# Binary convolution branch in jobs of 784 pixels on all four 64x64 corners of TensorE, with a scalar operand in the ratio

## Chip, core and metric

One NeuronCore of a Trainium2 chip runs the whole program. The metric is the time of one execution on the device in microseconds (us); lower is better.

## What is computed

The input `x` is (32, 64, 56, 56) in float32. Two blocks follow each other, each with a residual. The first is a binary convolution branch: the signs of the group-normed input go through a 3x3 depthwise convolution with sign weights, PReLU, batch norm and sign, a 1x1 convolution with sign weights, PReLU and batch norm. The second is an involution: a 1x1 convolution (64 to 576 channels, float32) makes nine filter taps per pixel, and these are multiplied with the nine shifted copies of the group-normed input and summed.

```python
def _L0(x):                       # x is already group-normed
    h = sign(x)
    h = depthwise3x3(h, sign(dw_weight))
    h = sign(bn1(prelu1(h)))
    h = einsum('bchw,oc->bohw', h, sign(pw_weight))
    return bn2(prelu2(h)) + x

def _L1(x):
    f = einsum('bchw,oc->bohw', x, W) + b        # 9 taps per channel
    return sum_k(patch_k(x) * f[:, :, k])

x = x + _L0(gn(x))                # gn: 32 groups of 2 channels
x = x + _L1(gn(x))
```

## The kernel before

A **tile** is two images, 128 partitions (image 0 on partitions 0 to 63, image 1 on 64 to 127, one channel per partition) by 3136 pixels. There are 16 tiles. The engines' programs are written by hand: a loop over steps, in each of which one tile is `taps` (its involution runs), the next one is `mid`, the one after that `front`, and one is being loaded. Inside a step there are 36 **units** `u`: four **quarters** of the image (784 pixels in two halves of 392), nine taps each. Every engine runs through the same units in order, and each piece of work has a unit at which it stands in an engine's queue; a delay such as `PW_DELAY` is a distance in units. Units count on from a step into the next, where `front` becomes `mid`.

**Involution.** For unit `u` TensorE (`unit`, L340) makes one tap of 784 pixels with four float32 matmuls, one in each 64x64 corner of the array (each stands as two records in the trace), into one of `SLOTS = 3` PSUM slots of `tap_ps`. VectorE (`product`, L667) adds the bias and multiplies it with the shifted `q`. Unit `u` may start only when product `u - 3` has ended (L347); where that product is the ninth tap of a quarter, it waits for `pair` (L692) instead, a sum that VectorE runs after the first product of the next quarter:

```python
before = t.count(UNITS, u - SLOTS)
if before % KK == PAIR_K:
    wait(pe, paired, before // KK + 1)
else:
    wait(pe, prod_done, before + 1)
```

Counting the units of a quarter from 0 to 8, `pair` stands behind product 0 of the next quarter, and unit 2 of that quarter waits for it. GpSimd sums the products of a quarter (L270 to L304), partly through an accumulating DMA.

**Convolution branch.** It works in 8 **chunks** of 392 pixels. For a chunk, TensorE runs nine depthwise taps of two matmuls (`depthwise`, L359), each in its own diagonal corner, so that both images run side by side, into `dw_ps`. ScalarE makes two sign planes `ab` from it (`conv_act`, L427). TensorE multiplies both with the 1x1 weights into `pw_ps` (`pointwise`, L375), ScalarE applies a ReLU in place (`relu_act`, L434), TensorE adds the planes once more (`add_h`, L384), and VectorE adds the result to `xb` in place with a sum for the next norm (`x1_sum`, L653). A chunk starts every 4 units; `dw_ps` and `pw_ps` are one bank each and `ab` has two buffers. In each engine's queue the piece for unit `u` of TensorE comes behind `unit(u)`, and `x1_sum` on VectorE comes ahead of `product(u)`.

**Statistics.** ScalarE makes the sums (`sum0`, `square0`, `sum1`, `square1`), VectorE exchanges partner channels with small shuffles, GpSimd takes the power. VectorE also makes `ratio` (L648), a 128x1 product of two operands in SBUF. `q_pass` and `q_half` on ScalarE write the normed `q`, and eight copies (`mirror_half`, L213) bring the other image's half to each side before the tile's taps start.

Of the kernel before, what the change touches and what calls it, by code (L numbers as in the profile page):

```python
# [18 lines left out]
def preact_involution_kernel(nc, x, dw, a1, gam1, bet1, mu1, var1, pw, a2, gam2, bet2, mu2, var2, W, b, out):  # L19
# [12 lines left out]
    SLOTS = 3  # L32
    N_GROUP = 2 * NPIX
# [8 lines left out]
    with ExitStack() as ctx:  # L42
# [8 lines left out]
        signs = sb("signs", [P, HP, WP], BF16)  # L51
# [34 lines left out]
        dw_ps = ctx.enter_context(nc.psum_tensor("dw_ps", [P, 512], F32))  # L86
        pw_ps = ctx.enter_context(nc.psum_tensor("pw_ps", [P, 512], F32))
# [13 lines left out]
        sums = sb("sums", [P, 2, CHUNKS], F32)  # L101
        scaled = sb("scaled", [P, CHUNKS], F32)
# [75 lines left out]
        def chunks_due(u, delay, mid, front):  # L178
            return due(u, delay, FIRST_CHUNK, CHUNK_EVERY, CHUNKS, front, mid)

# [140 lines left out]
        def _(pe):  # L321
            pe.wait_ge(ident_ready, 1)
            pe.wait_ge(signs_ready, 3)
            pe.matmul(dw_ps[:, 0:P], pw_block[:], ident_bf[:], start=True, stop=True)
            pe.matmul(dw_ps[:, P:2 * P], pw_block[:], ident_sg[:], start=True, stop=True).then_inc(pw_turned, 1)
            pe.wait_ge(pwk_ready, 1)
            pe.matmul(pw_ps[:, 0:1], pw_k[:], minus_k_terms[:], start=True, stop=True).then_inc(k_ready, 1)
# [31 lines left out]
            def depthwise(t, c, taps):  # L359

                if c == 0 and taps.start == 0:
# [12 lines left out]

            def pointwise(t, c):  # L375
                pe.wait_ge(ab_done, t.count(CHUNKS, c + 1))
                wait(pe, x1_done, t.count(CHUNKS, c))
                for n, pw_n in enumerate((pw_a, pw_b)):
                    for side in range(2):
                        own = slice(side * C, side * C + C)  # L380
                        mm = pe.matmul(pw_ps[own, 0:CH], pw_n[own, own], ab[own, c % 2, n, :], start=(n == 0), stop=(n == 1))  # L381
                mm.then_inc(pw_ready, 1)

            def add_h(t, c):  # L384

                pe.wait_ge(relu_done, t.count(CHUNKS, c + 1))
                for n, pw_n in enumerate((pw_a_sg, pw_b_sg)):
                    for side in range(2):
                        own = slice(side * C, side * C + C)
                        mm = pe.matmul(pw_ps[own, 0:CH], pw_n[own, own], ab[own, c % 2, n, :], start=False, stop=(n == 1),  # L390
                                       skip_group_check=True)
                mm.then_inc(h_ready, 1)

            def step(done, taps, mid, front, load):
                for u in range(UNITS):
# [6 lines left out]
                    for t, c in chunks_due(u, 0, mid, front):  # L402
                        depthwise(t, c, range(0, 5))
                    for t, c in chunks_due(u, 1, mid, front):
                        depthwise(t, c, range(5, KK))
                    for t, c in chunks_due(u, PW_DELAY, mid, front):
                        pointwise(t, c)
                    for t, c in chunks_due(u, ADD_H_DELAY, mid, front):
                        add_h(t, c)
# [4 lines left out]
        def _(act):  # L414
# [12 lines left out]
            def conv_act(t, c):  # L427

                act.wait_ge(dw_ready, t.count(CHUNKS, c + 1))
                wait(act, h_ready, t.count(CHUNKS, c - 1))  # L430
                acts(ab[:, c % 2, 0, :], dw_ps[:, 0:CH], ACT.Sign, scale=c_(A_SC), bias=c_(A_BI))
                acts(ab[:, c % 2, 1, :], dw_ps[:, 0:CH], ACT.Sign, scale=c_(B_SC), bias=c_(B_BI)).then_inc(ab_done, 1)

            def relu_act(t, c):  # L434
                act.wait_ge(pw_ready, t.count(CHUNKS, c + 1))
                acts(pw_ps[:, 0:CH], pw_ps[:, 0:CH], ACT.Relu, scale=c_(NEG_D), bias=c_(NEG_DK)).then_inc(relu_done, 1)
# [12 lines left out]
            def sum1(t):  # L449

                act.wait_ge(x1_done, t.count(CHUNKS, CHUNKS))
# [16 lines left out]
            def sign0(t):  # L468
                wait(act, dw_ready, t.count(CHUNKS))
                acts(signs[:, 1:1 + H, 1:1 + WD], rows3(xb[:, t.slot, :]), ACT.Sign, bias=s_(t, NM0)).then_inc(signs_done, 1)  # L470

            def scales0(t):
# [8 lines left out]
                acts(s_(t, HALF_B), s_(t, ZB), ACT.Copy, scale=-0.5 / CHUNKS)  # L481
# [30 lines left out]
            def step(done, taps, mid, front, load):  # L512
                for u in range(UNITS):
                    for t, c in chunks_due(u, AB_DELAY, mid, front):
                        conv_act(t, c)
                    for t, c in chunks_due(u, PW_DELAY, mid, front):
                        relu_act(t, c)
# [271 lines left out]
```

## Time and profile before

| what | value |
|---|---|
| median of 3 runs | 834.75 us (833.67 to 837.43) |
| the profiled execution | 835.78 us, its span 833.9 us |
| VectorE busy | 747.3 us, 90% |
| TensorE busy | 702.7 us, 84% |
| GpSimd busy | 573.4 us, 69% |
| ScalarE busy | 518.5 us, 62% |

The span has three stretches. Up to 88.6 us there is no involution work: tile 0 and part of tile 1 go through the convolution branch. From 88.6 to 761.9 us 58 quarters of the involution run with convolution work beside them. The last 6 quarters, up to 823.1 us, have none, and 11 us of closing work follow. Busy shares over the whole span mix these.

### The profile page before, as it was taken

To read this page: it belongs to the slowest core of one execution; us is meant where nothing else is said; L and a number is where in the kernel's file an instruction comes from. 1 tells how busy PE (TensorE), PEld (TensorE's weight loads), DVE (VectorE), ACT (ScalarE), POOL (GpSimd) and SP (SyncE) were. 2 spreads that over 40 slices of the span, in tenths; PEclk is the share of its full clock that TensorE was granted. 3 is DMA by queue.
4 is the path that set the end of the run, shared out by engine and by line. 5 is a ranking of instruction groups with operands and counts; after the bars stand their busy time and mean duration, and the time that the engine had idled before them with its cause. 6 is when DMAs were issued, how large, how long until landed. Compare 5 with 4: busy or idle time off the path is not lost.

```text
span 833.9 us, 19099 instructions
## 1 busy us (share of the span) xinstructions
PE 702.7 (84%) x7975; PEld 404.2 (48%) x7975; DVE 747.3 (90%) x1136; ACT 518.5 (62%) x772; POOL 573.4 (69%) x393
## 2 busy tenths in 40 slices
PE   0766889899998989998999989998999989897783
PEld 0323556455555555554555555554555555552221
DVE  6211799999999999999999999999999999999998
ACT  4586876667676767667685767766675767633000
POOL 2000167878787787878687786878787777778885
PEclk9988999999999999999999999999999999999986
DMA  5101559798887979698888889697988888686983
GB/s 205 44 1 31 140 115 248 149 210 192 173 219 160 235 147 246 139 233 170 210 182 173 215 163 247 140 238 159 217 180 171 212 172 165 142 174 143 198 165 95
DMA packets 40023, 142.14 MB, mean 170 GB/s; under 512 B 5248, under 2 KB 13440, under 8 KB 37888
## 3 DMA queue, kind: packets, MB, share of 16 engines
q0 software_dynamic: 17296, 75.87, 50.7%
q1 hardware_dynamic: 22640, 65.04, 23.4%
q8 instruction: 63, 1.03, 0.5%
q14 instruction: 24, 0.20, 0.1%
HBM read 25.86 MB, written 25.69 MB: 62 GB/s over the span
## 4 chain that ended last, share of the span: by engine, by line
DVE 56%; PE 32%; issue 6%; ACT 5%; DMA 1%; SPq 0%; DVEq 0%
DVE prod L685 35%; PE tap_ps L356 18%; PE dw_ps L369 11%; DVE prod L697 7%; DVE tap_ps L685 6%; DVE xb L659 4%; PE pw_ps L390 2%; ACT ab L416 2%; DVE st L651 1%; ACT unused L416 1%; PE pw_ps L381 1%; DVE st L555 1%; DMA prod<-prod 1%; ACT signs L416 1%; DVE prod L705 0%
## 5 line engine op out<-in xcount | busy, mean ns | idle before, releaser
L356 PE MATMUL tap_ps<-q,w_t 64*64 64x392 f32 x2304 | 466.9, 500 | 63.6 <-DVE prod L697 61.3
L356 PE MATMUL tap_ps<-mirror,w_t 64*64 64x392 f32 x2304 | 479.9, 517 | 0.0
L685 DVE SCALAR_TENSOR_TENSOR prod<-tap_ps,bias,q 128x784 f32<-128x784 f32 x448 | 452.3, 1029 | 11.5 <-PE tap_ps L356 7.3
L369 PE MATMUL dw_ps<-signs,dw_diag 64*64 64x392 bf16 x2304 | 246.3, 335 | 16.0 <-ACT ab L416 13.6
L416 ACT ACTIVATE ab<-dw_ps,col 128x392 bf16<-128x392 f32 x256 | 158.5, 669 | 160.0 <-PE dw_ps L369 160.0
L356 PEld LDWEIGHTS tap_ps<-q,w_t 64*64 64x64 f32 x2304 | 171.8, 134 | 166.9 <-DVE prod L697 95.8
L369 PEld LDWEIGHTS dw_ps<-signs,dw_diag 64*64 64x64 bf16 x2304 | 146.3, 108 | 139.2 <-issue 81.4
L282 POOL TENSOR_TENSOR prod<-prod 128x784 f32<-128x784 f32 x63 | 117.0, 1857 | 90.3 <-DVE prod L697 90.3
L289 POOL TENSOR_TENSOR prod<-prod 128x784 f32<-128x784 f32 x63 | 139.7, 2218 | 27.6 <-DMA prod<-prod 27.6
L356 PEld LDWEIGHTS tap_ps<-mirror,w_t 64*64 64x64 f32 x2304 | 124.6, 133 | 2.2
L304 POOL TENSOR_TENSOR ob<-prod 128x784 f32<-128x784 f32 x63 | 116.8, 1854 | 10.6 <-POOL prod L295 10.3
L295 POOL TENSOR_TENSOR prod<-prod 128x784 f32<-128x784 f32 x63 | 116.5, 1849 | 0.0
L659 DVE SCALAR_TENSOR_TENSOR xb<-pw_ps,st,xb 128x392 f32<-128x392 f32 x128 | 79.1, 618 | 39.8 <-PE pw_ps L390 39.2
L274 POOL DMA_DIRECT2D prod<-prod x63 | 76.4, 1213 | 54.3 <-DVE prod L685 54.3
L416 ACT ACTIVATE pw_ps<-pw_ps,col 128x392 f32<-128x392 f32 x128 | 82.7, 646 | 30.7 <-PE pw_ps L381 30.7
L416 ACT ACTIVATE unused<-xb,st 128x3136 bf16<-128x3136 f32 x32 | 94.6, 2955 | 1.1
L685 DVE SCALAR_TENSOR_TENSOR tap_ps<-tap_ps,bias,q 128x784 f32<-128x784 f32 x64 | 66.3, 1036 | 4.1 <-PE tap_ps L356 4.1
L685 DVE SCALAR_TENSOR_TENSOR prod<-tap_ps,st,q 128x784 f32<-128x784 f32 x64 | 65.9, 1030 | 4.4 <-PE tap_ps L356 4.0
L697 DVE SCALAR_TENSOR_TENSOR prod<-tap_ps,st,prod 128x784 f32<-128x784 f32 x64 | 65.7, 1026 | 0.0
L381 PE MATMUL pw_ps<-ab,pw_a 64*64 64x392 bf16 x256 | 44.9, 331 | 14.2 <-ACT ab L416 9.8
L416 ACT ACTIVATE q<-xb,st 128x1568 f32<-128x1568 f32 x32 | 52.6, 1692 | 0.5
L259 POOL TENSOR_SCALAR st<-st 128x1 f32<-128x1 f32 x32 | 9.5, 297 | 56.4 <-DVE st L555 53.6
(101 smaller groups left out, 464.2 us busy)
## 6 DMA issues: line engine op xcount, KB each, us to landing
prod<-prod POOLq DMA_DIRECT2D x63, 1176.0 KB, 10.3
xb<-in_x_dram SPq DMA_DIRECT2D x16, 1568.0 KB, 11.7
out_dram<-ob SPq DMA_DIRECT2D x64, 392.0 KB, 2.9
mirror<-q SPq DMA_DIRECT2D x128, 101.5 KB, 4.6
prod<-prod SPq DMA_DIRECT2D x1, 146.2 KB, 2.3
prod<-in_L_conv_W_dram SPq DMA_DIRECT2D x1, 144.0 KB, 6.3
prod<-prod SPq DMA_DIRECT2D x1, 20.8 KB, 6.1
prod<-in_L_conv_prelu_a_dram SPq DMA_DIRECT2D x1, 0.2 KB, 2.3
```

Source lines behind the costliest of these rows:

```text
L274: pool.dma_start(prod[:, g % BUFS, 3:6, :], prod[:, g % BUFS, 0:3, :], accum_op=ALU.add, max_dma_last_dim=6 * QP).then_inc(folded[g % BUFS ...
L282: pool.tensor_tensor(pr[6], pr[6], pr[7], ALU.add).then_inc(summed67, 1)
L289: pool.tensor_tensor(pr[4], pr[4], pr[5], ALU.add).then_inc(summed45, 1)
L295: pool.tensor_tensor(pr[3], pr[3], pr[6], ALU.add).then_inc(summed36, 1)
L304: pool.tensor_tensor(ob[:, qq % 2, :], pr[3], pr[4], ALU.add).then_inc(summed, 1)
L356: mm = pe.matmul(rows3(tap_ps[to, u % SLOTS, side, 0:CH]), w_t[own, k, :], moving, start=True, stop=True)
L369: mm = pe.matmul(rows3(dw_ps[own, 0:CH]), dw_diag[own, k, own], signs[own, c * ROWS + dy:c * ROWS + dy + ROWS, dx:dx + WD], start=(k == 0) ...
L381: mm = pe.matmul(pw_ps[own, 0:CH], pw_n[own, own], ab[own, c % 2, n, :], start=(n == 0), stop=(n == 1))
L416: return nc.scalar.activation(o, i, f, **kw)
L659: v.scalar_tensor_tensor(xc, pw_ps[:, 0:CH], s_(t, RATIO), xc, ALU.mult, ALU.add, accum_out=sums[:, t.par, c:c + 1]).then_inc(x1_done, 1)
L685: v.scalar_tensor_tensor(place.rearrange("p j (a b) -> p j a b", b=WD), psum.rearrange("p j (a b) -> p j a b", b=WD), s_(t, B4) if k == 4 ...
L697: v.scalar_tensor_tensor(into, tap_ps[:, (KK * g + PAIR_K) % SLOTS, :, 0:CH], s_(t, MEAN1), into, ALU.add, ALU.add).then_inc(paired, 1)
```

## The change

The branch works in 4 **jobs** of 784 pixels instead of 8 chunks of 392. A job is two chunks. In `depthwise` the image picks the rows of the array and the PSUM bank, and the chunk picks the columns, that is the output partitions: all four corners work on one tap, with the same number of matmuls in all. In `pointwise` and `add_h` the roles are exchanged back: the chunk picks rows and bank, the image the columns. One PSUM tensor `conv_ps` of two banks takes the place of `dw_ps` and `pw_ps` and serves a job from its first depthwise tap to `x1_sum`; `ab` has one buffer. ScalarE and VectorE work on 784 pixels per instruction. Each job's nine taps stand in three units instead of two. `signs` has a buffer for each parity of the tile. `ratio` takes its second operand as a per-partition scalar. The places of all pieces in the queues are new.

```diff
-        dw_ps = ctx.enter_context(nc.psum_tensor("dw_ps", [P, 512], F32))
-        pw_ps = ctx.enter_context(nc.psum_tensor("pw_ps", [P, 512], F32))
+        conv_ps = ctx.enter_context(nc.psum_tensor("conv_ps", [P, 2, 512], F32))
...
-            def depthwise(t, c, taps):
+            def depthwise(t, j, taps):
...
                 if taps.start == 0:
-                    wait(pe, ab_done, t.count(CHUNKS, c))
+                    wait(pe, x1_done, t.count(JOBS, j))
                 for k in taps:
                     dy, dx = divmod(k, 3)
-                    for side in range(2):
-                        own = slice(side * C, side * C + C)
-                        mm = pe.matmul(rows3(dw_ps[own, 0:CH]), dw_diag[own, k, own],
-                                       signs[own, c * ROWS + dy:c * ROWS + dy + ROWS, dx:dx + WD],
-                                       start=(k == 0), stop=(k == KK - 1))
+                    for image in range(2):
+                        own = slice(image * C, image * C + C)
+                        for chunk in range(2):
+                            to = slice(chunk * C, chunk * C + C)
+                            first = (2 * j + chunk) * ROWS + dy
+                            mm = pe.matmul(rows3(conv_ps[to, image, 0:CH]), dw_diag[own, k, own],
+                                           signs[own, t.par, first:first + ROWS, dx:dx + WD],
+                                           start=(k == 0), stop=(k == KK - 1))
...
+                pe.wait_ge(ab_done, t.count(JOBS, j + 1))
                 for n, pw_n in enumerate((pw_a, pw_b)):
+                    for chunk in range(2):
+                        own = slice(chunk * C, chunk * C + C)
+                        for image in range(2):
+                            to = slice(image * C, image * C + C)
+                            mm = pe.matmul(conv_ps[to, chunk, 0:CH], pw_n[own, own], ab[own, n, image, :],
+                                           start=(n == 0), stop=(n == 1))
...
+                    for part in range(3):
+                        for t, j in jobs_due(u, part, mid, front):
+                            depthwise(t, j, range(3 * part, 3 * part + 3))
...
-                v.tensor_tensor(s_(t, RATIO), s_(t, INVZ), c_(S2_SG), ALU.mult).then_inc(ratio_done, 1)
+                v.tensor_scalar(s_(t, RATIO), s_(t, INVZ), c_(S2_SG), None, ALU.mult).then_inc(ratio_done, 1)
...
-                v.scalar_tensor_tensor(xc, pw_ps[:, 0:CH], s_(t, RATIO), xc, ALU.mult, ALU.add,
-                                       accum_out=sums[:, t.par, c:c + 1]).then_inc(x1_done, 1)
+                xj = xb[:, t.slot, j * QP:(j + 1) * QP].rearrange("p (a n) -> p a n", a=2)
+                v.scalar_tensor_tensor(xj, conv_ps[:, :, 0:CH], s_(t, RATIO), xj, ALU.mult, ALU.add,
+                                       accum_out=sums[:, t.par, j:j + 1]).then_inc(x1_done, 1)
...
-FIRST_CHUNK = 13
-CHUNK_EVERY = 4
-PW_DELAY = 6
-AB_DELAY = 2
-X1_DELAY = 9
-ADD_H_DELAY = 8
+FIRST_JOB = 20
+JOB_EVERY = 9
+AB_DELAY = 3
+PW_DELAY = 5
+RELU_DELAY = 6
+ADD_H_DELAY = 7
+X1_DELAY = 5
...
-SUM1_AT = 18
-MEAN1_AT = 15
-SQUARE1_AT = 18
+SUM1_AT = 19
+MEAN1_AT = 18
+SQUARE1_AT = 20
 VAR1_AT = 21
-R1_AT = 23
-Q_AT = (23, 26)
+R1_AT = 22
+Q_AT = (27, 28)
```

## Rows read from the trace of the kernel before

**Rows 1.** Busy us (x instructions), clock, DMA share, GB/s, by stretch.

```profile
core 0: us, PE busy (x) PEld busy (x) DVE busy (x) ACT busy (x) POOL busy (x), PEclk, DMA share, GB/s
33.00:55.00 22.00, 14.49 (x150) 7.30 (x146) 4.01 (x16) 15.55 (x22) 0.29 (x1) 1.00 0.00 1
...
100.00:740.00 640.00, 581.81 (x6835) 348.92 (x6830) 624.73 (x922) 441.21 (x661) 491.99 (x327) 1.00 0.83 188
```

**Rows 2.** Groups of instructions: busy us, mean ns of one, idle before.

```profile
L685 DVE SCALAR_TENSOR_TENSOR prod<-tap_ps,bias,q 128x784 f32<-128x784 f32 x448 | 452.3, 1029 | 11.5 <-PE tap_ps L356 7.3
L416 ACT ACTIVATE ab<-dw_ps,col 128x392 bf16<-128x392 f32 x256 | 158.5, 669 | 160.0 <-PE dw_ps L369 160.0
L659 DVE SCALAR_TENSOR_TENSOR xb<-pw_ps,st,xb 128x392 f32<-128x392 f32 x128 | 79.1, 618 | 39.8 <-PE pw_ps L390 39.2
L416 ACT ACTIVATE pw_ps<-pw_ps,col 128x392 f32<-128x392 f32 x128 | 82.7, 646 | 30.7 <-PE pw_ps L381 30.7
L416 ACT ACTIVATE unused<-xb,st 128x3136 bf16<-128x3136 f32 x32 | 94.6, 2955 | 1.1
...
L665 DVE RECIPROCAL st<-st 128x1 f32<-128x1 f32 x16 | 2.4, 153 | 0.0
```

**Rows 3.** VectorE in order of time: start us, us, what.

```profile
307.02 0.62 DVE L659 SCALAR_TENSOR_TENSOR xb<-pw_ps,st,xb 128x392 f32<-128x392 f32 x1
...
307.56 1.04 DVE L685 SCALAR_TENSOR_TENSOR tap_ps<-tap_ps,bias,q 128x784 f32<-128x784 f32 x1
...
309.56 1.03 DVE L697 SCALAR_TENSOR_TENSOR prod<-tap_ps,st,prod 128x784 f32<-128x784 f32 x1
310.50 2.13 DVE L685 SCALAR_TENSOR_TENSOR prod<-tap_ps,bias,q 128x784 f32<-128x784 f32 x2
```

**Rows 4.** TensorE in order of time, the same place.

```profile
310.63 0.54 PE L356 MATMUL tap_ps<-q,w_t 64*64 64x392 f32 x1 [1.17 <-DVE prod L697]
310.64 0.55 PE L356 MATMUL tap_ps<-mirror,w_t 64*64 64x392 f32 x2
...
311.35 1.02 PE L369 MATMUL dw_ps<-signs,dw_diag 64*64 64x392 bf16 x10
...
312.19 0.33 PE L390 MATMUL pw_ps<-ab,pw_a_sg 64*64 64x392 bf16 x1
...
315.17 0.51 PE L356 MATMUL tap_ps<-q,w_t 64*64 64x392 f32 x2
...
315.83 0.51 PE L356 MATMUL tap_ps<-q,w_t 64*64 64x392 f32 x2
```

**Rows 5.** The ratio's instruction alone: duration ns min/median/max.

```profile
L651 DVE TENSOR_TENSOR st<-st,col x16: 160/1794/1809, 24.8 to 717.6; 128x1 f32<-128x1 f32 x16
```

**Rows 6.** VectorE: the first products, and the sums L697 that close quarters.

```profile
88.62 1.98 DVE L685 SCALAR_TENSOR_TENSOR prod<-tap_ps,bias,q 128x784 f32<-128x784 f32 x2 [1.45 <-PE tap_ps L356]
...
760.87 1.03 DVE L697 SCALAR_TENSOR_TENSOR prod<-tap_ps,st,prod 128x784 f32<-128x784 f32 x1
...
801.92 1.03 DVE L697 SCALAR_TENSOR_TENSOR prod<-tap_ps,st,prod 128x784 f32<-128x784 f32 x1
...
812.34 1.03 DVE L697 SCALAR_TENSOR_TENSOR prod<-tap_ps,st,prod 128x784 f32<-128x784 f32 x1
```

**Rows 7.** TensorE in a late quarter without convolution work.

```profile
803.00 0.54 PE L356 MATMUL tap_ps<-q,w_t 64*64 64x392 f32 x1 [1.94 <-DVE prod L697]
...
804.40 0.87 PE L356 MATMUL tap_ps<-mirror,w_t 64*64 64x392 f32 x2
...
805.06 0.87 PE L356 MATMUL tap_ps<-mirror,w_t 64*64 64x392 f32 x2
```

**Rows 8.** The same quarter by stretches, columns as in rows 1.

```profile
804.00:806.00 2.00, 2.00 (x16) 0.81 (x13) 1.63 (x2) 0.00 (x0) 2.00 (x2) 0.50 1.02 179
```

**Rows 9.** TensorE: the first chunk's taps and the first tap unit.

```profile
23.31 3.15 PE L369 MATMUL dw_ps<-signs,dw_diag 64*64 64x392 bf16 x18 [2.13 <-ACT signs L416]
...
87.45 0.55 PE L356 MATMUL tap_ps<-mirror,w_t 64*64 64x392 f32 x2
```

More of the change, by code:

```diff
@@ L50, in preact_involution_kernel @@
         xb = sb("xb", [P, RING, NPIX], F32)
-        signs = sb("signs", [P, HP, WP], BF16)
+        signs = sb("signs", [P, 2, HP, WP], BF16)
         q = sb("q", [P, 2, HP, WP], F32)
@@ L372, in depthwise, with pointwise @@
                 if taps.stop == KK:
                     mm.then_inc(dw_ready, 1)
-            def pointwise(t, c):
-                pe.wait_ge(ab_done, t.count(CHUNKS, c + 1))
-                wait(pe, x1_done, t.count(CHUNKS, c))
+            def pointwise(t, j):
+                pe.wait_ge(ab_done, t.count(JOBS, j + 1))
                 for n, pw_n in enumerate((pw_a, pw_b)):
-                    for side in range(2):
-                        own = slice(side * C, side * C + C)
-                        mm = pe.matmul(pw_ps[own, 0:CH], pw_n[own, own], ab[own, c % 2, n, :], start=(n == 0), stop=(n == 1))
+                    for chunk in range(2):
[4 more added lines that the diff above has]
+                                           start=(n == 0), stop=(n == 1))
@@ L382, in pointwise, with add_h @@
                 mm.then_inc(pw_ready, 1)
-            def add_h(t, c):
-                pe.wait_ge(relu_done, t.count(CHUNKS, c + 1))
+            def add_h(t, j):
+                pe.wait_ge(relu_done, t.count(JOBS, j + 1))
                 for n, pw_n in enumerate((pw_a_sg, pw_b_sg)):
[L388 to L391, printed above, removed]
+                    for chunk in range(2):
+                        own = slice(chunk * C, chunk * C + C)
+                        for image in range(2):
+                            to = slice(image * C, image * C + C)
+                            mm = pe.matmul(conv_ps[to, chunk, 0:CH], pw_n[own, own], ab[own, n, image, :],
+                                           start=False, stop=(n == 1), skip_group_check=True)
@@ L401, in step @@
                         unit(taps, u)
[L402 to L409, printed above, removed]
+                    for part in range(3):
+                        for t, j in jobs_due(u, part, mid, front):
+                            depthwise(t, j, range(3 * part, 3 * part + 3))
+                    for t, j in jobs_due(u, PW_DELAY, mid, front):
+                        pointwise(t, j)
+                    for t, j in jobs_due(u, ADD_H_DELAY, mid, front):
+                        add_h(t, j)
             program(step)
@@ L425, in s_, with conv_act, relu_act @@
                 return st[:, t.slot, n:n + 1]
[L427 to L436, printed above, removed]
+            def conv_act(t, j):
+                act.wait_ge(dw_ready, t.count(JOBS, j + 1))
+                acts(ab[:, 0, :, :], conv_ps[:, :, 0:CH], ACT.Sign, scale=c_(A_SC), bias=c_(A_BI))
+                acts(ab[:, 1, :, :], conv_ps[:, :, 0:CH], ACT.Sign, scale=c_(B_SC), bias=c_(B_BI)).then_inc(ab_done, 1)
+            def relu_act(t, j):
+                act.wait_ge(pw_ready, t.count(JOBS, j + 1))
+                acts(conv_ps[:, :, 0:CH], conv_ps[:, :, 0:CH], ACT.Relu, scale=c_(NEG_D), bias=c_(NEG_DK)).then_inc(relu_done, 1)
             def sum0(t):
@@ L468, in sign0 @@
             def sign0(t):
-                wait(act, dw_ready, t.count(CHUNKS))
-                acts(signs[:, 1:1 + H, 1:1 + WD], rows3(xb[:, t.slot, :]), ACT.Sign, bias=s_(t, NM0)).then_inc(signs_done, 1)
+                wait(act, dw_ready, t.count(JOBS, -JOBS))
+                acts(signs[:, t.par, 1:1 + H, 1:1 + WD], rows3(xb[:, t.slot, :]), ACT.Sign, bias=s_(t, NM0)).then_inc(signs_done, 1)
             def scales0(t):
@@ L513, in step @@
                 for u in range(UNITS):
[L514 to L517, printed above, removed]
+                    for t, j in jobs_due(u, AB_DELAY, mid, front):
+                        conv_act(t, j)
+                    for t, j in jobs_due(u, RELU_DELAY, mid, front):
+                        relu_act(t, j)
                     if front:
@@ L717, in step @@
                         copy_w()
-                    for t, c in chunks_due(u, X1_DELAY, mid, front):
-                        x1_sum(t, c)
+                    for t, j in jobs_due(u, X1_DELAY, mid, front):
+                        x1_sum(t, j)
                     if taps:
```

52 lines of the change are left out of this document (26 added, 26 removed).

## Prediction

> **What bounds the kernel now.** I read the stretches first: from 100 to 740 us VectorE is busy for 624.73 of 640 us, 97.6%, more than any other engine [rows 1]. So in the long middle each microsecond that VectorE works or waits is one of the result; ScalarE (441) and TensorE (582, ends modelled) matter only where VectorE waits for them. Then I took prices from the groups [rows 2] and spacings from the order of time [rows 3, 4], because neighbours on VectorE overlap: x1_sum lasts 0.62 us but the next product starts 0.54 behind it; `pair` starts at 309.56 and the next product at 310.50, so both cost 0.94. The middle runs from 88.62 to the end of the `pair` at 760.87, 761.89: 58 quarters, 673.3 us, **11.61 us a quarter** [rows 6]. Of that, 9 x 0.943 + 0.945 + 2 x 0.54 = 10.5 is product, pair and x1_sum; the rest is small instructions, the ratio above all, and waits.
>
> **What it saves.** x1_sum: a product of 784 elements costs 0.41 us more than an x1_sum of 392 (1029 against 618 ns, both with a PSUM and an SBUF operand [rows 2]), so one of 784 costs 0.54 + 0.41 = 0.95 in place of 1.08: 0.13 a quarter. Ratio: 1794 ns in the median, 160 at its shortest [rows 5]. With a scalar operand only one tensor comes from SBUF; the nearest row with one such input is the reciprocal, 153 ns also in the middle [rows 2], so I take 0.15: 1.6 us a tile. Bounds: 0.15 and the old 1.8. The Trainium skill (SBUF — State Buffer, Who interferes with whom) says that VectorE's second read port is shared with GpSimd and that tensor_scalar can enter a mode that uses it; by that the ratio would still be held, and the sum would be some 15 us higher (an estimate: 14 tiles in the middle by 1.6 us, of which VectorE's waits at that place cover about a third). No row here has a tensor_scalar beside a busy GpSimd.
>
> TensorE: a depthwise tap of one chunk costs (312.19 - 311.35)/5 = 0.168 us for two corners [rows 4]. The tap units start matmuls in several corners within 0.01 us of each other (310.63, 310.64) and a whole unit of eight records takes 315.83 - 315.17 = 0.66 [rows 4], so four corners do run side by side in float32. I take 0.168 for four bf16 corners as well, bounds 0.168 and 0.336. A third of a job's taps is then 0.50, a pointwise or add_h of two passes 0.33. This halves TensorE's convolution work, but by itself is worth nothing while VectorE is the bound. ScalarE: (2955 - 669)/2744 = 0.83 ns an element [rows 2], so 392 more cost 0.33: the sign pair of a job 1.90 us, the ReLU 0.97.
>
> **What it adds: a wait in VectorE's own queue.** In units from a job's start, x1_sum now stands ahead of product 5, so VectorE comes to it when product 4 has ended. What it needs is add_h, which stands on TensorE behind unit 7. And unit 7 may start only when product 4 has ended. So VectorE stands still while TensorE runs unit 7 and add_h, whatever their speed. Before, x1_sum stood ahead of product 9 and add_h behind unit 8, which needs product 5 only: three products in between covered it. Behind the waiting x1_sum lie all products, and TensorE's unit 8 waits for them.
>
> I follow one quarter, with time 0 at the end of a `pair` and k the tap in the quarter. Jobs start at k = 2. Prices: TensorE starts 0.04 behind the release, a unit from rest holds it 0.72 (310.63 to 311.35), and VectorE can start 0.25 after a unit's stream (310.50 + 2.13 - 1.03 = 311.60 against 311.35) [rows 3, 4].
> - Unit 2 streams till 0.76; product 2 starts at 1.01, 0.15 later than back to back. The x2 row of 2.13 us shows this wait today.
> - Third of the taps 1.26, unit 3 till 1.92, product 3 at 2.16: waits 0.21. Third, unit 4 till 3.08, product 4 at 3.32: 0.22. Third till 3.58, unit 5 till 4.24, product 5 at 4.48: 0.22. Product 6 follows back to back and ends at 6.45.
> - Signs 3.80 to 5.70; units 6 and 7 stream till 5.56; pointwise till 6.07; ReLU 6.30 to 7.27; unit 8 till 6.73; the next quarter's unit 0 needs product 6 and streams till 7.40; add_h till 7.73; x1_sum starts at 7.98 instead of 6.37: **it waits 1.6 us**.
> - x1_sum, products 7, 8, 0 and `pair` end at 12.79. Check: 9 x 0.943 + 0.945 + 0.95 + 0.80 + 1.61 = 12.8.
>
> The small instructions fall mostly at k = 1 to 3, where VectorE waits for TensorE anyway: nothing. var1 now stands three products behind mean1, with square1 (3.0 us and small ones) between: some 0.6 us, of which 0.2 reach x1_sum; once a tile, left out.
>
> **The clock.** TensorE now rests from 7.73 to 9.91 and from about 10.6 to 12.8, with one unit between. In the late quarters, where it rests 1.94 us in one go at the same place [rows 7], the granted clock falls behind it: 0.50, that is 1.2 GHz, in the stretch from 804 to 806 [rows 8], and unit starts lie 1.32 us apart (two passes of 0.66) instead of 0.66 [rows 4, 7]. There VectorE bears most of it: 10.42 us from pair to pair [rows 6] against 9.6 by the sum without x1_sum. With conv work TensorE is the bound from 0 to 8 us, so a low stretch there costs half its length. A 3.3 us stretch (803.7 to 807) costs at most 1.65, at least nothing where it falls in the rests. The new rests are longer than the one that lowers the clock now, so it can fall earlier, partly inside them: I take 0.9, the middle. The quarter is then 13.7.
>
> The Trainium skill (TensorE: Matmul & The Clock Gate, Why this matters for your kernels) warns of one idle gap between bursts, of a length that neither rest reaches; by that rule the clock holds. The trace of the late quarters disagrees: there a shorter rest was enough.
>
> **The start.** The first tap unit starts at 87.45 [rows 9]. Until then the branch runs without involution, limited by its own chain. Warm, a job is taps 1.7, signs 1.9, pointwise 0.5, ReLU 1.0, add_h 0.5, x1_sum 1.0: 6.7 us, like two chunks now. Cold (3.15 us for 9 taps at 23.31 [rows 9]) it is 9. But less of it stands ahead of the first tap unit: tile 0's four jobs (23.3 to 58.5, one waiting for tile 1's signs), sum and square (63), tile 1's first signs and ReLU (67), `q` (71) and its copies. I get the first unit at 77 to 79: **9 us less**, bounds 5 and 12. The last 6 quarters and the close don't change.
>
> **The sum.** The profiled execution took 835.8 (span 833.9; the median of the runs is 1 lower). 58 x (13.7 - 11.61) = +121, start -9: 948; I say 947 for the median.
>
> **Rivals.**
> - A, as above: x1_sum waits and the clock falls in each quarter. 920 to 975. Chance 0.70.
> - B, the clock holds (the page's rule; also, from 33 to 55 us TensorE is busy 14.5 of 22 us with rests and stays at 1.00 [rows 1]): 58 x (12.8 - 11.61) = +69, -9: 895. Against it: the late quarters. 0.14.
> - C, bf16 taps in four corners don't run fully side by side. With 0.336 a tap each third grows by 0.5, the waits at k = 3 to 5 and the job's chain by 1.5 in all: 58 x 1.5 = 87 above A, 1034; halfway 990. Or the low clock costs its full 1.65: 990 too. Against it: float32 units do run together [rows 4]. 0.09.
> - D, thirds of taps come for nothing and x1_sum waits only its least, 0.04 + 0.72 + 0.33 + 0.25 from product 6's end, 1.42: quarter 10.4 + 0.15 + 1.42 = 11.95, +20 - 9 = 847. 0.03.
> - E, not slower: VectorE never waits at x1_sum, because TensorE is further ahead than the slot rule lets me think. Place: x1_sum of each job; price: 1.6 us and the long rests with it; the quarter is 11.2, 58 x -0.4 - 9 = 803. It decides from a quarter of 11.77 down, a wait of about 0.5. Nothing in the trace speaks for it. 0.04.
>
> **Numbers.** 947, likeliest range 920 to 975. To hold 8 in 10 it takes in B and the lower part of C: 888 to 980. A measurement can tell 0.5% (4 us) from no change; faster 0.04 (E), same 0.02 (the low edge of D), slower 0.94.
>
> **What would show it.** In the trace after: about 60 waits of VectorE at L659's successor for add_h, 1.3 to 1.7 us each, near 95 us in all; products at k = 3 to 5 spaced 1.16 us or more; pair to pair 13.7; TensorE's mean clock well under 0.976, with a low stretch in nearly every quarter; ratio 0.15 us; x1_sum near 1.03; first tap unit near 78. Pairs 12.8 apart with clock 1.00 mean B; under 11.8 means my reading of the queues is wrong. `q` is also written later against its copies; if a tile's first unit waits for them, each microsecond costs 14 us more.

## The result, and the profile after

| | before | after |
|---|---|---|
| median (lowest to highest), us | 835.3 (833.7 to 837.4) | 1012.1 (1009.7 to 1012.2) |
| ratio, 95% interval | | 1.210 (1.206 to 1.214) |
| profiled execution, its span, us | 835.8, 833.9 | 1009.7, 1007.8 |
| mean granted clock of TensorE | 0.976 | 0.841 |

Slower, by 177 us; the forecast was 947 (888 to 980). One more execution of the kernel after took 1111 us at a clock of 0.668 and is left out of the table.

Stretches of the kernel after: three quarters one by one (from the end of one `pair` to the end of the next), then the middle. Columns as in [rows 1].

```profile
270.47:284.97 14.50, 10.44 (x124) 4.76 (x124) 10.91 (x17) 4.81 (x11) 9.49 (x7) 0.87 0.55 113
284.97:299.27 14.30, 10.17 (x124) 4.33 (x124) 11.15 (x18) 10.48 (x13) 9.50 (x7) 0.86 0.56 114
299.27:314.86 15.59, 11.53 (x124) 4.82 (x124) 10.90 (x14) 5.99 (x6) 8.57 (x5) 0.82 0.91 242
100.00:740.00 640.00, 462.68 (x5364) 199.18 (x5364) 474.27 (x639) 320.39 (x392) 391.36 (x259) 0.85 0.67 152
```

VectorE, busy for 97.6% of this stretch before, is now busy for 474.27 of 640 us, 74%, and no other engine is busier. No engine is the bound any more: they wait for each other. The three quarters, 14.5, 14.3 and 15.6 us, repeat to the end of the middle, and none of them has the clock at 1.00.

The waits of the kernel after, by engine and line: us in total, times, longest.

```profile
DVE xb L664 <- PE conv_ps L397: 128.4, 64, 7.7
DVE prod L690 <- PE tap_ps L356: 127.7, 161, 1.3
PE tap_ps L356 <- DVE prod L690: 122.6, 58, 2.2
PE tap_ps L356 <- DVE prod L702: 121.5, 63, 1.9
```

The first is x1_sum waiting for add_h (before: 39.8 us, of which 39.2 before 90 us [rows 2]); 87.8 us of it lie in the middle, 57 times 1.54. The second is a product waiting for its tap unit. The last two are TensorE's two rests in each quarter, up to 2.2 and 1.9 us long. One quarter of it, VectorE first, then TensorE:

```profile
310.05 1.03 DVE L664 SCALAR_TENSOR_TENSOR xb<-conv_ps,st,xb 128x784 f32<-128x784 f32 x1 [1.52 <-PE conv_ps L397]
...
313.84 1.02 DVE L702 SCALAR_TENSOR_TENSOR prod<-tap_ps,st,prod 128x784 f32<-128x784 f32 x1
314.78 1.02 DVE L690 SCALAR_TENSOR_TENSOR prod<-tap_ps,bias,q 128x784 f32<-128x784 f32 x1
316.27 1.03 DVE L690 SCALAR_TENSOR_TENSOR prod<-tap_ps,bias,q 128x784 f32<-128x784 f32 x1 [0.47 <-PE tap_ps L356]
...
318.63 1.03 DVE L690 SCALAR_TENSOR_TENSOR prod<-tap_ps,bias,q 128x784 f32<-128x784 f32 x1 [1.25 <-PE tap_ps L356]
319.95 1.03 DVE L690 SCALAR_TENSOR_TENSOR prod<-tap_ps,st,q 128x784 f32<-128x784 f32 x1 [0.29 <-PE tap_ps L356]
```

```profile
309.66 0.34 PE L397 MATMUL conv_ps<-ab,pw_b_sg 64*64 64x392 bf16 x4
312.09 0.54 PE L356 MATMUL tap_ps<-q,w_t 64*64 64x392 f32 x1 [2.10 <-DVE prod L690]
...
314.92 0.62 PE L356 MATMUL tap_ps<-q,w_t 64*64 64x392 f32 x1 [1.94 <-DVE prod L702]
...
318.27 0.89 PE L372 MATMUL conv_ps<-signs,dw_diag 64*64 64x392 bf16 x12
318.97 0.49 PE L356 MATMUL tap_ps<-q,w_t 64*64 64x392 f32 x1
...
319.63 0.68 PE L372 MATMUL conv_ps<-signs,dw_diag 64*64 64x392 bf16 x12
320.14 0.49 PE L356 MATMUL tap_ps<-q,w_t 64*64 64x392 f32 x1
```

add_h's last matmuls start at 309.66; x1_sum, which stood waiting for 1.52 us, starts at 310.05 and releases TensorE, which has rested 2.10 us, only through the product behind it; a second rest of 1.94 us follows at the `pair`. In this quarter the granted clock falls behind that, at 315.25. A third of the taps takes 0.51 us in the high clock (319.63 to 320.14), and between 300 and 303.5 us, where the next row has the clock at 0.50, it takes 0.98 (300.68 to 301.66):

```profile
300.00:303.50 3.50, 3.50 (x36) 1.65 (x32) 1.48 (x4) 0.29 (x1) 3.33 (x3) 0.50 0.83 190
```

```profile
300.68 1.20 PE L372 MATMUL conv_ps<-signs,dw_diag 64*64 64x392 bf16 x12
301.66 0.86 PE L356 MATMUL tap_ps<-q,w_t 64*64 64x392 f32 x1
```

The first product, and the last `pair` with convolution work behind it, in the order of time of the kernel after:

```profile
78.05 2.91 DVE L690 SCALAR_TENSOR_TENSOR prod<-tap_ps,bias,q 128x784 f32<-128x784 f32 x3
...
935.04 1.02 DVE L702 SCALAR_TENSOR_TENSOR prod<-tap_ps,st,prod 128x784 f32<-128x784 f32 x1
```

From 78.05 to 936.06 there are 58 quarters of 14.79 us, where there were 58 of 11.61 from 88.62 [rows 6]. 58 x 3.18 = +184.4, the start -10.6: +174 us, which is what the profiled executions differ by. The question is what the 3.18 us are.

### The profile page after: what moved, and what is told of

The parts are those of the page before. It is cut to its first block, busy times and chain, and to the rows that moved or that the text cites. A ratio compares the mean times of both kernels' runs of the same rounds, so it can differ in the third digit from the quotient of the medians.

```text
span 1007.8 us, 18526 instructions
## 1 busy us (share of the span) xinstructions
PE 699.7 (69%) x7975; PEld 296.9 (29%) x7975; DVE 727.1 (72%) x1008; ACT 475.8 (47%) x580; POOL 574.3 (57%) x393
## 4 chain that ended last, share of the span: by engine, by line
PE 60%; DVE 28%; issue 6%; ACT 4%; DMA 1%; SPq 1%; DVEq 0%
PE tap_ps L356 40%; DVE prod L690 14%; PE conv_ps L372 14%; DVE prod L702 6%; DVE tap_ps L690 6%; PE conv_ps L385 3%; PE conv_ps L397 2%; DVE xb L664 2%; ACT unused L422 1%; ACT ab L422 1%; DMA prod<-prod 1%; ACT signs L422 1%; ACT conv_ps L422 0%; DVE prod L710 0%; SPq L192 0%
## 5 line engine op out<-in xcount | busy, mean ns | idle before, releaser
L356 PE MATMUL tap_ps<-q,w_t 64*64 64x392 f32 x2304 | 538.2, 574 | 245.8 <-DVE prod L690 122.6
L356 PE MATMUL tap_ps<-mirror,w_t 64*64 64x392 f32 x2304 | 533.9, 574 | 0.0
L422 ACT ACTIVATE ab<-conv_ps,col 128x784 bf16<-128x784 f32 x128 | 121.6, 1000 | 284.8 <-PE conv_ps L372 284.8
L372 PE MATMUL conv_ps<-signs,dw_diag 64*64 64x392 bf16 x2304 | 180.2, 431 | 8.1 <-DVE xb L664 6.0
L356 PEld LDWEIGHTS tap_ps<-mirror,w_t 64*64 64x64 f32 x2304 | 167.4, 151 | 1.8 <-issue 1.7
L664 DVE SCALAR_TENSOR_TENSOR xb<-conv_ps,st,xb 128x784 f32<-128x784 f32 x64 | 66.1, 1034 | 128.4 <-PE conv_ps L397 128.4
L372 PEld LDWEIGHTS conv_ps<-signs,dw_diag 64*64 64x64 bf16 x2304 | 95.0, 145 | 152.5 <-issue 122.4
L304 POOL TENSOR_TENSOR ob<-prod 128x784 f32<-128x784 f32 x63 | 116.7, 1852 | 10.6 <-POOL prod L295 10.3
L422 ACT ACTIVATE conv_ps<-conv_ps,col 128x784 f32<-128x784 f32 x64 | 62.6, 977 | 41.8 <-PE conv_ps L385 41.8
L422 ACT ACTIVATE st<-st 128x1 f32<-128x1 f32 x176 | 36.0, 236 | 56.2 <-DVE st L560 51.0
L422 ACT ACTIVATE signs<-xb,st 128x3136 bf16<-128x3136 f32 x16 | 46.4, 2898 | 0.0
```

Of the source, the lines that this page charges most:

```text
L304: pool.tensor_tensor(ob[:, qq % 2, :], pr[3], pr[4], ALU.add).then_inc(summed, 1)
L356: mm = pe.matmul(rows3(tap_ps[to, u % SLOTS, side, 0:CH]), w_t[own, k, :], moving, start=True, stop=True)
L372: mm = pe.matmul(rows3(conv_ps[to, image, 0:CH]), dw_diag[own, k, own], signs[own, t.par, first:first + ROWS, dx:dx + WD], start=(k == 0), ...
L422: return nc.scalar.activation(o, i, f, **kw)
L664: v.scalar_tensor_tensor(xj, conv_ps[:, :, 0:CH], s_(t, RATIO), xj, ALU.mult, ALU.add, accum_out=sums[:, t.par, j:j + 1]).then_inc(x1_done, 1)
```

## Experiments

The theory (some of the expectations call it theory Q) is the forecast's: x1_sum waits for a matmul that cannot run before the product ahead of it has ended, this costs the quarter up to 12.8 us, and the rest is TensorE's clock, which falls in the rests so made. Ratios are to the kernel before on the same chip. Where an expectation counts x1_sum's units "behind add_h's", they are counted in the code from the job's start: `X1_DELAY` 5, 6 and 7 put x1_sum ahead of the job's product 5, 6 and 7, and add_h stays behind unit 7. So 0, 1 and 2 products lie between x1_sum and the one that releases add_h's unit, and 2 in the retimed kernel (both delays 4).

**x1_sum two products later.** The computation is whole.

```diff
-X1_DELAY = 5
+X1_DELAY = 7
```

> The changed kernel with X1_DELAY = 7 instead of 5: x1_sum stands behind two more products in VectorE's queue, nothing else moves. Theory Q (the queue places make VectorE wait at x1_sum, and the rests that this gives TensorE lower its clock): the 1.52 us waits at x1_sum go, 58 of them or 88 us, and part of the low clock with them; quarter 11.2 to 12.9 instead of 14.8, total 800 to 890. Rival J (the job's own chain on four corners and one PSUM tensor is what costs, wherever x1_sum stands): the wait only moves to another instruction, total 980 or more.

Measured: 861.4 us, ratio 1.031 (1.028 to 1.035). One constant gives back 151 of the 177 us. The waits at x1_sum are gone from the middle. TensorE now has one rest of 2.65 us in each quarter. The quarters are of two kinds: 33 of 57 take 12.9 us in a lower mean clock, the others 11.2 (a few 11.6) in the high one. Four of them in a row:

```profile
274.33:287.20 12.87, 10.20 (x124) 4.85 (x124) 10.82 (x15) 6.71 (x7) 8.55 (x5) 0.87 1.03 274
287.20:298.40 11.20, 8.53 (x124) 4.10 (x124) 10.82 (x17) 6.43 (x11) 9.49 (x7) 1.00 0.61 130
298.40:311.27 12.87, 10.20 (x124) 4.84 (x124) 11.08 (x18) 10.40 (x13) 9.53 (x7) 0.87 0.69 139
311.27:322.48 11.21, 8.67 (x124) 4.08 (x124) 10.82 (x15) 6.08 (x7) 8.63 (x5) 1.00 0.88 178
```

The same work takes 11.20 us with the clock at 1.00 and 12.87 at a mean of 0.87: a low stretch costs 1.67 us.

**x1_sum one product later.**

```diff
-X1_DELAY = 5
+X1_DELAY = 6
```

> The kernel after with x1_sum's unit 6 units behind add_h's (5 in the kernel after, 7 in the run with late x1_sum). Theory (the wait is the distance in products to the add that it needs, and the clock falls in the rests of TensorE beside it): the wait of 1.52 us shrinks by about one product to 0.4 to 0.6 us, the clock lies between 0.85 and 0.91 in the middle, total 880 to 930. Rival (the wait is gone with the first product of distance): 861, as with 7.

Measured: 934.2 us, ratio 1.118 (1.116 to 1.120), a little over the expected. The wait is 0.6 us and the usual quarter 13.56. Three of 57 quarters nearly kept the clock (0.98 and 0.99) and took 11.9 to 12.2 us. So the first product of distance gives 78 us and the second 73.

**The same wait put into the kernel before.** x1_sum stands 6 units behind its chunk (7 for a job's third chunk), where add_h is not out; the reciprocal and the ratio move ahead with it.

```diff
-                    for t, c in chunks_due(u, X1_DELAY, mid, front):
-                        x1_sum(t, c)
+                    for delay in (X1_DELAY, X1_DELAY + 1):
+                        for t, c in chunks_due(u, delay, mid, front):
+                            if (c == 2) == (delay > X1_DELAY):
+                                x1_sum(t, c)
...
-X1_DELAY = 9
+X1_DELAY = 6
...
-INV_Z_AT = 19
-RATIO_AT = 20
+INV_Z_AT = 18
+RATIO_AT = 18
```

> The kernel before (chunks, two corners, two PSUM banks) with x1_sum put 6 units behind the chunk's start instead of 9 (7 for the one chunk where 6 can't work), so that like in the changed kernel add_h comes on TensorE behind a tap unit that waits for the product just ahead of x1_sum; inv_z and ratio are 1 and 2 units earlier. Theory Q: VectorE waits 1.3 us or more at most of the 8 chunks of a tile, 14 tiles, so +110 to +170 us, and more if the clock falls: 940 to 1060. Rival J (the cost belongs to the jobs on four corners): within 10 us of 835.

Measured: 1114.5 us, ratio 1.334 (1.330 to 1.338). Waits of the kernel before with this edit:

```profile
DVE xb L659 <- PE pw_ps L390: 339.7, 128, 7.3
```

The mechanism is the same and needs neither jobs of 784 pixels nor four corners. Its size was missed: 2.65 us a wait in the mean, 2.5 in the middle (282.4 us, 112 times), where 1.3 or more was expected. The order of time shows what else stands in it: behind the tap unit that VectorE has just released come five taps of a later chunk, and add_h only behind them:

```profile
403.82 0.55 PE L356 MATMUL tap_ps<-mirror,w_t 64*64 64x392 f32 x2
...
404.52 1.02 PE L369 MATMUL dw_ps<-signs,dw_diag 64*64 64x392 bf16 x10
405.36 0.35 PE L390 MATMUL pw_ps<-ab,pw_a_sg 64*64 64x392 bf16 x2
```

```profile
405.92 0.63 DVE L659 SCALAR_TENSOR_TENSOR xb<-pw_ps,st,xb 128x392 f32<-128x392 f32 x1 [2.16 <-PE pw_ps L390]
```

The taps alone are 405.36 - 404.52 = 0.84 us of the 2.16. The two longest waits between 400 and 440 us, 3.8 and 4.4 us, follow on units that TensorE runs in the low clock.

**The scalar operand alone, in the kernel before.**

```diff
-v.tensor_tensor(s_(t, RATIO), s_(t, INVZ), c_(S2_SG), ALU.mult)
+v.tensor_scalar(s_(t, RATIO), s_(t, INVZ), c_(S2_SG), None, ALU.mult)
```

> The kernel before with the ratio by a scalar operand alone. If a single SBUF tensor frees it from GpSimd: 0.2 us instead of 1.79, 14 to 16 times, of which waits of today may eat a part: 810 to 822. If tensor_scalar is held like tensor_tensor was: 835 and 1.8 us in the trace.

Measured: 821.1 us, ratio 0.984 (0.980 to 0.988): 14 us faster, as expected.

**The two-tensor form back in the kernel after.** The reverse of that edit.

> The kernel after with the ratio computed as a product of two tiles again, as in the kernel before. It leaves the computation whole. The ratio is then an instruction of about 1.8 us instead of 0.20 us, once in 13 to 14 us of work on VectorE per tile's quarter in which it stands. Theory (VectorE sets the pace, and the scalar operand saves 1.6 us in each of 16 tiles): 13 to 26 us slower than the kernel after. Rival (it stands where VectorE waits for taps anyway): 0 to 5 us slower.

Measured: 1009.8 us, ratio 1.207 (1.203 to 1.212): no slower than the kernel after (1012.1), as the rival had it. The scalar operand is worth 14 us where VectorE is the bound and nothing where VectorE waits behind it.

**The rest behind add_h filled.** 16 sets of four matmuls of 120 columns that nothing reads, into columns of PSUM that nothing uses, behind the unit that follows add_h.

```diff
+            def fill(t, j):
+                pe.wait_ge(x1_done, t.count(JOBS, j + 1))
+                for _ in range(FILL):
+                    for chunk in range(2):
+                        own = slice(chunk * C, chunk * C + C)
+                        for image in range(2):
+                            to = slice(image * C, image * C + C)
+                            pe.matmul(conv_ps[to, chunk, CH:CH + 120], pw_a[own, own], ident_bf[own, 0:120],
+                                      start=True, stop=True)
...
+                    for t, j in jobs_due(u, ADD_H_DELAY + 1, mid, front):
+                        if taps:
+                            fill(t, j)
...
+FILL = 16
```

> The changed kernel with 16 sets of four 64x64 matmuls of 120 columns each put behind the tap unit that follows add_h, into columns of conv_ps that nobody reads; they work in the rest of TensorE before pair and are added work only. Theory Q with the clock as the missing part of the prediction: the granted clock stays near 1.00, the quarter falls from 14.8 to about 12.8, total about 890 to 920. Rival: the excess over 12.8 us is not the clock's (taps or units simply take longer in four corners): total 1000 or more, since work was added.

Measured: 943.6 us, ratio 1.129 (1.126 to 1.132). The waits at x1_sum stayed (127.4 us), 3776 matmuls were added to TensorE, and the kernel became 68 us faster than the one after. It was expected faster still: the rest of 2.1 us ahead of that unit remained, and the clock was 0.88 from 100 to 740 us, not 1.00.

**Both rests filled, short matmuls.** 8 sets ahead of that unit and 20 behind it.

```diff
+                    for t, j in jobs_due(u, ADD_H_DELAY + 1, mid, front):
+                        if taps:
+                            fill(t, j, FILL_A)
                     if taps:
                         unit(taps, u)
...
+                    for t, j in jobs_due(u, ADD_H_DELAY + 1, mid, front):
+                        if taps:
+                            fill(t, j, FILL_B)
...
+FILL_A, FILL_B = 8, 20
```

The filling waits for x1_sum, whose result stands in the same PSUM tensor, so of the first rest only what follows x1_sum is filled. 57 rests of 1.2 us remain ahead of it.

> The kernel after, with matmuls that nothing reads in both rests of TensorE: 8 sets of four 64x120 matmuls ahead of the unit that follows add_h (the one that waits for x1_sum) and 20 sets behind it. The waits of VectorE at x1_sum stay (64 waits, some 1.5 us each). Theory (what the quarter has over 12.8 us is TensorE's lower clock): granted clock near 1.00 from 95 us on, quarters of about 12.8 us, total about 895 (885 to 905), less than the kernel with the filling behind the unit alone (943.6). Rival (the excess over 12.8 us is waits that do not hang on the clock): clock up, total 940 or more.

Measured: 947.3 us, ratio 1.133 (1.129 to 1.138). By the total this is the rival's number. But the clock was 0.99 from 100 to 740 us, and the quarters fell into two kinds: 31 of 57 at 12.8 to 13.1 us, 23 of them at 12.82, and 26 longer ones of up to 18.6. In 22 of these TensorE stood still between matmuls with nothing to wait for ("issue"):

```profile
275.69 0.66 PE L372 MATMUL conv_ps<-signs,dw_diag 64*64 64x392 bf16 x9
278.90 0.53 PE L372 MATMUL conv_ps<-signs,dw_diag 64*64 64x392 bf16 x3 [2.55 <-issue]
```

So this run could not decide.

**Both rests filled, long matmuls.** The same filling in 36 matmuls of 392 columns per job, where there were 112 of 120: 3 sets ahead of the unit and 6 behind it.

```diff
-                            pe.matmul(conv_ps[to, chunk, CH:CH + 120], pw_a[own, own], ident_bf[own, 0:120],
+                            pe.matmul(conv_ps[to, chunk, 0:CH], pw_a[own, own], ab[own, 0, image, :],
...
-FILL_A, FILL_B = 8, 20
+FILL_A, FILL_B = 3, 6
```

> The kernel after with both rests of TensorE filled as before, but by matmuls of 392 columns: 3 sets of four ahead of the unit that follows add_h and 6 sets behind it, 36 matmuls per job where the run with both rests filled by 120 columns had 112. That run had a granted clock of 1.00 in nearly all of the middle and quarters of 12.82 us, but also quarters of 13.1 to 18.6 in which TensorE stood 2 us and more with nothing that the profile shows to wait for. Theory (those stops are the price of the many added instructions, and the loss over 12.8 us in the kernel after is the clock): quarters of 12.8 to 13.0 nearly throughout, total 895 to 905. Rival (the stops belong to the order of the kernel after, and the clock explains only part): total 930 or more.

Measured: 905.1 us, ratio 1.083 (1.081 to 1.086). Three quarters in a row, and the middle:

```profile
289.64:302.46 12.82, 10.45 (x160) 4.96 (x160) 10.91 (x15) 8.33 (x7) 8.57 (x5) 1.00 0.98 209
302.46:315.27 12.81, 10.45 (x160) 5.03 (x160) 10.91 (x17) 4.81 (x11) 9.46 (x7) 1.00 0.56 117
315.27:328.35 13.08, 10.67 (x160) 4.91 (x160) 10.99 (x18) 10.43 (x13) 9.49 (x7) 1.00 0.62 127
100.00:740.00 640.00, 521.61 (x7944) 245.90 (x7936) 542.38 (x735) 369.68 (x455) 446.35 (x297) 1.00 0.76 172
```

Three of four quarters take 12.82 us and the fourth 13.08, without exception. The wait of 1.5 us at x1_sum is in all of them, the low clock in none. TensorE does 36 matmuls more in each and the kernel is 107 us faster. The forecast's 12.79 us for a quarter in the high clock stands, and the 14.79 - 12.88 = 1.9 us above it in the kernel after went when the clock was held. The stops of the run before this one are gone too. The matmuls are fewer here, but also longer, with another input and another place in PSUM, so that it was their number is likely but not shown.

**Late x1_sum with its rest filled.** X1_DELAY 7, and 18 sets of 120 columns, or 6 sets of 392, behind the unit that follows add_h.

```diff
+                    for t, j in jobs_due(u, ADD_H_DELAY + 1, mid, front):
+                        if taps:
+                            fill(t, j, FILL_B)
...
+FILL_A, FILL_B = 0, 18
...
-X1_DELAY = 5
+X1_DELAY = 7
```

> The kernel after with x1_sum's unit 7 units behind add_h's instead of 5, and 18 sets of four matmuls that nothing reads in the rest of 2.65 us that TensorE then has ahead of the pair. Theory (the two lengths of quarter of the kernel with late x1_sum alone, 11.2 and 12.9 us, are the two levels of the clock): granted clock near 1.00, every quarter about 11.2 us, total 800 to 810, faster than the kernel before. Rival (the job form alternates for another reason): total stays near 860.

> The kernel with x1_sum's unit 7 units behind add_h's and the rest ahead of the pair filled, by 6 sets of four matmuls of 392 columns in place of 18 sets of 120 columns (823.6 us, quarters of 11.2 to 12.7). Theory (the quarters above 11.2 to 11.6 there were stops of TensorE beside its many instructions): 11.2 to 11.6 in all, total 808 to 815. Rival: 823 as with the short matmuls.

Measured: 823.6 us, ratio 0.985 (0.981 to 0.990), and 818.4 us, ratio 0.980 (0.977 to 0.982). Both are faster than the kernel before and both miss their forecasts, by 14 and by 3 us. The clock is at 1.00 from 100 to 700 us, and most quarters take 11.2 or 11.6 us, but 13 of 57 take up to 12.7, and with the long matmuls 9 of 57 up to 12.4. With the short matmuls TensorE has 8 such stops ("issue"), 5.0 us in all; with the long ones it has none, as expected, so the stops were only part of it. The 9 long quarters that remain are all the last of their tile. In each of them x1_sum waits again, 0.4 to 1.1 us. In five of them TensorE's first unit of the next tile, behind which add_h stands, waits 0.8 to 1.3 us for the copies of its `q`, and x1_sum with it; what holds the other four by 0.4 us is open:

```profile
534.77 0.51 PE L356 MATMUL tap_ps<-q,w_t 64*64 64x392 f32 x1 [1.25 <-DMA mirror<-q]
```

```profile
536.04 1.03 DVE L677 SCALAR_TENSOR_TENSOR xb<-conv_ps,st,xb 128x784 f32<-128x784 f32 x1 [1.11 <-PE conv_ps L397]
```

The last sentence of the forecast names this wait. It came here and in the retimed kernels; in the kernel after TensorE never waits for these copies in the middle.

**The same jobs, retimed.** Nothing is filled, and the computation is whole. All nine taps of a job stand in one piece behind one unit, each further step at least one product behind what it needs, and the small sums of a tile move with them.

```diff
-                    for part in range(3):
-                        for t, j in jobs_due(u, part, mid, front):
-                            depthwise(t, j, range(3 * part, 3 * part + 3))
+                    for t, j in jobs_due(u, 0, mid, front):
+                        depthwise(t, j, range(0, KK))
...
-FIRST_JOB = 20
+FIRST_JOB = 19
...
-AB_DELAY = 3
-PW_DELAY = 5
-RELU_DELAY = 6
-ADD_H_DELAY = 7
-X1_DELAY = 5
+AB_DELAY = 1
+PW_DELAY = 2
+RELU_DELAY = 3
+ADD_H_DELAY = 4
+X1_DELAY = 4
...
```

> The four-corner jobs kept, and only the order changed: all nine taps of a job in one piece behind the unit of product 1, the remaining units of the branch each placed at least one product behind what they need (x1_sum four units behind add_h), the first job one place earlier. Theory (the loss of the change is in its order alone: waits at x1_sum and the clock that falls in the rests they cause): no wait at x1_sum in the middle, granted clock near 1.00, quarters of 10.5 to 10.7 us, total 775 to 800. Rival (the job form itself costs time, on VectorE or in the exchange between partitions): 835 or more.

Measured: 796.0 us (786.1 to 800.5), ratio 0.948 (0.941 to 0.955): 5% faster than the kernel before and 21% than the one after. The middle, and VectorE's busy time in the page:

```profile
100.00:740.00 640.00, 535.00 (x7128) 224.15 (x7120) 623.34 (x853) 408.77 (x502) 527.29 (x349) 0.99 0.87 198
```

```profile
PE 607.8 (77%) x7975; PEld 253.0 (32%) x7975; DVE 710.0 (91%) x1008; ACT 474.1 (60%) x580; POOL 575.1 (73%) x393
```

VectorE is the bound again (97.4% busy), and no wait at x1_sum is left in the middle. The profiled execution was the fastest, 786.1 us, 50 us under that of the kernel before: 11 us of this lie ahead of the first `pair` (90.56 against 101.69 at its end) and 39 in the 57 quarters behind it. That is about what VectorE has less to do, 747.3 - 710.0 = 37 us, of which the ratio's instruction is 22 (16 times 1591 - 206 ns in the mean) and the x1_sums are the rest. No profile shows where the usual executions lose their further 10 us. In this one TensorE still waits 12 times for the copies of `q`, 13.6 us in all, and VectorE 10.5 us for tap units:

```profile
338.78 0.51 PE L356 MATMUL tap_ps<-q,w_t 64*64 64x392 f32 x1 [2.27 <-DMA mirror<-q]
```

**The two-tensor form in the retimed kernel.**

> The retimed kernel with the ratio as a product of two tiles again. There VectorE does not wait in the middle (10.5 us of waits between 95 and 715 us), so the 1.6 us of each of 16 tiles should now count: theory 14 to 26 us slower than the retimed kernel (the scalar operand alone gave 13 to 15 us in the kernel before); rival, as in the kernel after, where it gave nothing: within 5 us of it.

Measured: 797.7 us (797.4 to 798.5), ratio 0.955 (0.953 to 0.956): within 2 us of the retimed kernel, whose own executions spread over 14. The theory asked for 14 or more, and fell, though VectorE waits for only 22.2 us here between 95 and 715 us. The ratio's instruction shows why, here and then in the kernel after with the same form (duration ns min/median/max; before it was 160/1794/1809 [rows 5]):

```profile
L657 DVE TENSOR_TENSOR st<-st,col x16: 147/151/292, 24.6 to 676.9; 128x1 f32<-128x1 f32 x16
```

```profile
L656 DVE TENSOR_TENSOR st<-st,col x16: 159/1100/1425, 24.7 to 879.0; 128x1 f32<-128x1 f32 x16
```

The same instruction takes 0.15, 1.10 or 1.79 us by the place at which the order puts it.

## Why the prediction was right and wrong

- **The wait at x1_sum: right.** Forecast 1.6 us per job, measured 1.5; one product of distance leaves 0.6, two leave none.
- **The quarter in the high clock: right.** 12.8 worked out, 12.82 and 13.08 measured once the clock is held (mean 12.88). That is 58 x (12.88 - 11.61) = 74 us of the loss; the forecast had 69.
- **The clock: the step that failed.** "I take 0.9, the middle", of bounds 0 and 1.65. Measured 14.79 - 12.88 = 1.9 us a quarter, 111 us of the loss where 52 were forecast. The step counted one low stretch of 3.3 us per quarter and let nearly half of its cost go in the rests. Its price for a low microsecond was right, its count and its overlap were not. From 100 to 740 us the clock is 0.85, so TensorE is in the low clock for (1 - 0.85) x 2 x 640 = 192 us, in 43.3 quarters: 4.4 us in each. In the three quarters shown above it is low from 270.9 to 274.3, from 284.5 to 287.9 and from 298.2 to 305.0, so a stretch lasts 3.4 us twice and 6.8 us the third time: four stretches' length in three quarters. The middle of the long one, and the high clock on its two sides:

```profile
288.00:298.00 10.00, 7.19 (x104) 2.95 (x96) 7.65 (x11) 7.63 (x11) 6.55 (x6) 1.00 0.53 115
298.50:304.50 6.00, 5.18 (x44) 2.44 (x48) 3.85 (x5) 0.29 (x1) 4.98 (x3) 0.50 0.84 179
305.50:315.00 9.50, 5.44 (x76) 2.02 (x72) 7.85 (x10) 5.70 (x5) 3.13 (x3) 1.00 0.99 287
```

  Of these 13.6 us only 1.6 fall in the rest at the `pair` (TensorE starts again at 270.52, 285.02 and 299.32). The other 3.4, 2.9 and 5.7 us fall where thirds of taps and tap units alternate and TensorE sets the pace, the waits for taps growing to 1.25 us. Half of them is 1.7, 1.5 and 2.8 us, and the quarters are 14.5, 14.3 and 15.6, that is 1.7, 1.5 and 2.8 over 12.82. The run with late x1_sum pays the same price, 1.67 for one stretch. The bound of 1.65 was read from late quarters without convolution work (before: 10.42 us in the low clock, 9.59 in one that kept the high one), where no stretch is doubled and one costs only 0.8. A bound that would have held is two low stretches at full price, 2 x 1.65 = 3.3 us, against a worst quarter of +2.8.
- **Rival B, the clock holds:** 895 forecast, 905 measured when it was made to hold, so its price was right and its condition was not. It rested beside this on the Trainium skill (TensorE: Matmul & The Clock Gate, Why this matters for your kernels), which warns of single idle gaps longer than any here. The trace does not agree: no rest in the middle is over 2.2 us and the clock falls in every quarter.
- **The ratio: right in price, wrong in worth.** 0.15 forecast, 0.20 measured, in the middle of the tiles each time inside an instruction of GpSimd. The Trainium skill (SBUF — State Buffer, Who interferes with whom) lets tensor_scalar take the shared port only when its operands meet conditions, and says that an instruction with at most one SBUF input outside that mode does not contend. The forecast left these conditions out; the trace agrees with the second sentence, and the 15 us did not come. The sum counted its gain of 1.6 us a tile within the quarters; in the kernel after it is worth nothing (1009.8 with the old form, 1012.1 with the new).
- **Taps on four corners: right.** 0.51 us for a third, three taps in twelve matmuls, and 0.50 forecast. Rival C's reason did not occur, though its totals, 990 and 1034, lie on either side of the result.
- **Sizes: right.** x1_sum 1.03 us; the start 10.6 us shorter (9 forecast); the last six quarters 10.2 us as before.
- **What the forecast did not say:** that the loss is in the order alone: with the same computation in another order it is gone. How much of the retimed kernel's gain is due to the jobs is not shown. The scalar operand alone gives the kernel before 14 us, and the chunks of 392 pixels were not retimed in the same way.

## What to carry to other kernels

When an instruction of the bounding engine is placed, count the products (the hand-overs) between it and the matmul that it needs, each of which is itself released by that engine: at zero distance x1_sum waited 1.5 us here (1.54 in the kernel after, 1.49 with the clock held), and 0.84 us more where other taps stood ahead of its matmul. Price the clock by what TensorE does in a whole period after the rest, at both levels, and take twice its low time as a case, because rests repeated in each period can keep the clock low for part of every period: two of about 2 us did so in every quarter, one of 2.65 in 33 of 57. Before judging a faster form of work, retime everything around it: here the same work gave 1012 and 796 us. And ask in which instruction the saved time would otherwise go: the scalar operand was worth 14 us in one order and nothing in two others.

## What the runs showed of the hardware

**A VectorE instruction that ends with GpSimd's.** In the kernel before, VectorE's ratio starts at 299.97 and ends 1.80 later, at 301.77; GpSimd's sum ends at 299.91 + 1.84 = 301.75:

```profile
299.97 1.80 DVE L651 TENSOR_TENSOR st<-st,col 128x1 f32<-128x1 f32 x1
```

```profile
299.91 1.84 POOL L295 TENSOR_TENSOR prod<-prod 128x784 f32<-128x784 f32 x1
```

With the two-tensor form back in the kernel after it is 346.48 + 1.10 = 347.58 beside 345.72 + 1.85 = 347.57. In both kernels this holds for all 14 ratios from 100 us on, within 0.04 us. In the retimed kernel it starts at 676.92, before GpSimd's sum does at 677.04, and takes 0.15. So the price of this form is what is left of GpSimd's sum of 784 elements. A GpSimd instruction of one element did not hold it: at 587.91 the ratio took 0.15 us, while one ran from 587.90 to 588.52. The scalar form takes 0.20 us at 109.59, in the middle of GpSimd's from 108.83 to 110.68:

```profile
109.59 0.20 DVE L656 TENSOR_SCALAR st<-st,col 128x1 f32<-128x1 f32 x1
```

```profile
108.83 1.85 POOL L295 TENSOR_TENSOR prod<-prod 128x784 f32<-128x784 f32 x1
```

**The low clock costs half of its time where TensorE sets the pace.** 3.4, 2.9 and 5.7 us of it, behind the rest, made the quarter 1.7, 1.5 and 2.8 us longer.

**Work that makes the kernel faster.** 9 added sets of four matmuls per quarter, which nothing reads, took the kernel after from 1012.1 to 905.1 us; with them the clock stayed at 1.00 from 100 to 740 us. **Many short matmuls have a price of their own:** with 112 added matmuls of 120 columns per job TensorE had 22 stops of up to 3.0 us with nothing to wait for; with 36 of 392 columns it had none, and the total was 42 us lower.
